# A four-layer attention kernel: maximum blocks of equal width, sums of two tiles in one run, three probability buffers, one buffer of rounded biases

## The reference

```python
x = x + attention_l(groupnorm(x))          # l = 0..3, 32 groups, no affine part

# attention_l, 12 heads of 16 channels, S = 2304 positions
q, k, v = split(x @ qkv_w + qkv_b)
attn = (q * scale) @ k.T + rel_h[..., :, None] + rel_w[..., None, :]   # rel_* = q . rel_pos tables
out = softmax(attn) @ v                    # per head
return concat_heads(out) @ proj_w + proj_b
```

## Time and profile before

| | us |
|---|---|
| median of 3 runs | 6808.28 (6807.99 to 6810.07) |
| profiled execution, span on the core | 6801.4 |
| PE busy | 6725.5 (99%) |
| DVE busy | 5454.7 (80%) |
| ACT busy | 4753.7 (70%) |
| POOL busy | 938.1 (14%) |
| mean granted PE clock | 0.996 of 2.4 GHz |

### The profile page before, as it was taken

How to read it: one execution, slowest core, us unless ns; L and a number is a source line. 1 busy time by engine, 2 the same in 40 slices (tenths; PEclk the granted TensorE clock), 3 DMA queues, 4 the chain that set the end, 5 groups by cost and what they waited for, 6 DMA issues and landing times.

```text
span 6801.4 us, 139326 instructions
## 1 busy us (share of the span) xinstructions
PE 6725.5 (99%) x53600; PEld 4245.8 (62%) x53600; DVE 5454.7 (80%) x9973; ACT 4753.7 (70%) x10225; POOL 938.1 (14%) x967
## 2 busy tenths in 40 slices
PE   7999999999999999999999999999999999999998
PEld 5666666666666666666665666666666666666664
DVE  7887888778887788877888778887888878888883
ACT  3776776767767777677776767767676676767775
POOL 2111010211112110121111210102101121101110
PEclk8999999999999999999999999999999999999999
DMA  6676676767677677667676766767677676777673
GB/s 164 148 156 152 137 160 138 163 151 142 152 144 168 144 143 156 149 158 149 142 155 149 158 143 143 161 145 166 140 144 157 147 165 138 143 152 156 144 154 88
DMA packets 306307, 1013.72 MB, mean 149 GB/s; under 512 B 107440, under 2 KB 196976, under 8 KB 215920
## 3 DMA queue, kind: packets, MB, share of 16 engines
q1 hardware_dynamic: 305648, 1004.81, 68.9%
HBM read 745.26 MB, written 255.69 MB: 147 GB/s over the span
## 4 chain that ended last, share of the span: by engine, by line
PE 96%; DMA 1%; DVE 1%; issue 0%; ACT 0%; SPq 0%; POOL 0%; DVEq 0%; ACTq 0%
PE work L805 30%; PE work L878 27%; PE work L796 27%; PE work L824 7%; PE work L843 3%; PE work L862 2%; PE work L851 1%; DMA moving<-rel_scratch 1%; DVE mpart L683 1%; PE work L830 0%; DVE xb L674 0%; ACT probs L561 0%; DMA back<-attention_scratch 0%; DVE hi L721 0%; PE work L835 0%
## 5 line engine op out<-in xcount | busy, mean ns | idle before, releaser
L683 DVE TENSOR_REDUCE mpart<-work 128x1 f32<-128x512 f32 (+1 forms) x8640 | 5088.7, 632 | 1079.7 <-PE work L805 1013.1
L561 ACT ACTIVATE probs<-work 128x512 f32<-128x512 f32 (+1 forms) x8640 | 4100.2, 564 | 866.6 <-PE work L796 852.1
L805 PE MATMUL work<-mkeys,hi 128*128 128x512 f32 (+1 forms) x8640 | 3404.1, 395 | 10.6 <-DVE mpart L683 8.8
L796 PE MATMUL work<-moving,keys 113*128 113x512 f32 (+1 forms) x8640 | 3299.9, 383 | 10.9 <-DMA moving<-rel_scratch 5.7
L805 PEld LDWEIGHTS work<-mkeys,hi 128*128 128x128 f32 x8640 | 1643.6, 190 | 622.4 <-DVE mpart L683 324.0
L878 PE MATMUL work<-probs,vall 128*17 128x288 f32 x27648 | 2013.1, 409 | 0.0
L796 PEld LDWEIGHTS work<-moving,keys 113*128 113x128 f32 x8640 | 1642.1, 190 | 362.3 <-ACT probs L561 39.2
L878 PEld LDWEIGHTS work<-probs,vall 128*17 128x17 f32 x27648 | 637.3, 96 | 846.8 <-ACT probs L561 358.3
L824 PEld LDWEIGHTS work<-image,tab 128*48 128x48 f32 x6912 | 401.6, 124 | 544.9 <-ACT probs L561 513.2
L490 POOL TENSOR_TENSOR full<-full,hi 128x384 f32<-128x384 f32 x576 | 583.5, 1016 | 938.7 <-DVE hi L721 937.6
L495 POOL TENSOR_TENSOR rden<-oraw,rden 128x576 f32<-128x576 f32 x96 | 137.1, 1428 | 3955.3 <-DMA rden<-inverse_scratch 3955.3
(11 more groups left out here) (42 smaller groups left out, 646.8 us busy)
## 6 DMA issues: line engine op xcount, KB each, us to landing
moving<-rel_scratch SPq DMA_DIRECT2D x1728, 144.0 KB
moving<-qk_scratch SPq DMA_DIRECT2D x288, 576.0 KB
rel_scratch<-hi SPq DMA_DIRECT2D x192, 432.0 KB, 5.7
rel_scratch<-full SPq DMA_DIRECT2D x192, 432.0 KB, 5.5
moving<-rel_scratch SPq DMA_DIRECT2D x288, 288.0 KB
image<-qk_scratch SPq DMA_DIRECT2D x384, 144.0 KB, 3.2
keys<-qk_scratch SPq DMA_DIRECT2D x192, 288.0 KB, 7.8
qk_scratch<-split_hi SPq DMA_DIRECT2D x144, 192.0 KB, 3.9
```

The source lines that it names most:

```text
L561: act.activation(probs[:, tile % RING, lo:up], bank[:, 0:up - lo], ACT.Exp).then_inc(act_read, 1)
L683: dve.tensor_reduce(mpart[:, u % 2, q, m:m + 1], bank[:, 0:MSPLIT[m][1] - MSPLIT[m][0]], AX.X, ALU.max)\
L796: pe.matmul(bank[:, 0:up - lo], tile_of(keys[0:K_ROWS, u % 2, :], c, third), moving[0:K_ROWS, slot_of(u, third)[0], lo:up], start=True, st ...
L805: pe.matmul(bank[:, 0:up - lo], hi[:, u % 2, q * P:(q + 1) * P], mkeys[:, u % 2, lo:up], start=True, stop=True).then_inc(for_dve, 1)
```

## The change

- `RING` goes from 2 to 3 and `hi` from two buffers to one, so the memory used stays the same.
- `MSPLIT` becomes five even blocks, 462 columns four times and 456 once, where it was 256 and then four times 512.
- `attend` runs at the end of even tiles only, for the two tiles before, in one run of 32 instructions.
- The rounding of biases moves from tiles 8 to 13 to tiles 8 to 12 and 14 (`HIGH_AT`), and waits for the store of the unit just before.
- SP stores `hi` in tile 15 (13 before) and `full` in tile 16 (14 before), there behind the loads of the next unit's last slot. The waits at line 540 and in `fullq_load` stay as they are.

```diff
-RING = 2
+RING = 3
-MSPLIT = SPLIT[-1:] + SPLIT[:-1]
+MAX_STEP = 2 * -(-N // (2 * MAXB))
+MSPLIT = [(MAX_STEP * i, min(MAX_STEP * (i + 1), N)) for i in range(MAXB)]
+HIGH_AT = (8, 9, 10, 11, 12, 14)
-        hi = sb("hi", [P, 2, N], F32R)
+        hi = sb("hi", [P, N], F32R)
...
-                    if t == 13 and u + 2 < UNITS:
+                    if t == 15 and u + 2 < UNITS:
                         sp.wait_ge(hi_ready, NB * (u + 3))
-                        rel_store(u + 2, hi[:, (u + 2) % 2, :].bitcast(F32), 0, rel_hi_stored)
+                        rel_store(u + 2, hi[:, :].bitcast(F32), 0, rel_hi_stored)
                     if t == 14 and 0 <= u + 1 < UNITS:
                         top_load(u + 1, 0)
-                    if t == 14 and u + 2 < UNITS:
-                        sp.wait_ge(lo_ready, NB * (u + 3))
-                        rel_store(u + 2, full[:, :], 1, rel_lo_stored)
...
                     if t == 16 and 0 <= u + 1 < UNITS:
                         slot_load(u + 1, 2)
                         top_load(u + 1, 2)
+                    if t == 16 and u + 2 < UNITS:
+                        sp.wait_ge(lo_ready, NB * (u + 3))
+                        rel_store(u + 2, full[:, :], 1, rel_lo_stored)
...
                 if r == 0:
                     dve.wait_ge(fullq_in, 32 * (u + 1))
-                    if u >= 2:
-                        dve.wait_ge(rel_hi_stored, 32 * (u - 1))
+                    if u >= 1:
+                        dve.wait_ge(rel_hi_stored, 32 * u)
...
-                        if 8 <= t < 14 and i == 2 and -2 <= u and u + 2 < UNITS:
-                            high(u + 2, t - 8)
+                        if i == 2 and t in HIGH_AT and -2 <= u and u + 2 < UNITS:
+                            high(u + 2, HIGH_AT.index(t))
...
-                        if i == SB and 0 < tile <= TILES * UNITS:
+                        if i == SB and tile % 2 == 0 and 0 < tile <= TILES * UNITS:
+                            attend(tile - 2)
                             attend(tile - 1)
```

More of the change, by code:

```diff
@@ L489, in low @@
                 pool.wait_ge(hi_ready, NB * u + r + 1)
-                pool.tensor_tensor(full[:, cols], full[:, cols], hi[:, u % 2, cols].bitcast(F32), ALU.subtract)\
+                pool.tensor_tensor(full[:, cols], full[:, cols], hi[:, cols].bitcast(F32), ALU.subtract)\
                     .then_inc(lo_ready, 1)
@@ L718, in high @@
                     dve.wait_ge(fullq_in, 32 * (u + 1))
-                    if u >= 2:
-                        dve.wait_ge(rel_hi_stored, 32 * (u - 1))
-                dve.tensor_copy(hi[:, u % 2, cols], full[:, cols]).then_inc(hi_ready, 1)
+                    if u >= 1:
+                        dve.wait_ge(rel_hi_stored, 32 * u)
+                dve.tensor_copy(hi[:, cols], full[:, cols]).then_inc(hi_ready, 1)
             def top(u):
@@ L804, in fill @@
                         pe.wait_ge(mkeys_in[u % 2], 32 * (u // 2 + 1))
-                    pe.matmul(bank[:, 0:up - lo], hi[:, u % 2, q * P:(q + 1) * P], mkeys[:, u % 2, lo:up],
+                    pe.matmul(bank[:, 0:up - lo], hi[:, q * P:(q + 1) * P], mkeys[:, u % 2, lo:up],
                               start=True, stop=True).then_inc(for_dve, 1)
```

## The result

| | before | after |
|---|---|---|
| median, us | 6808.55 | 7757.0 (7748.0 to 7773.0) |
| ratio to before, 95% interval | | 1.1398 (1.1384 to 1.1412) |
| span of the profiled execution, us | 6801.4 | 7750.8 |
| mean granted PE clock | 0.996 | 0.953 |

The account below looks back on a forecast made before the run. PE was taken to bound the kernel, with 96% of the span as its work, DVE next. 6808 + 50 (pairs) + 670 (store wait) + 232 (clock) = 7760 us, chance 0.56; range 7140 to 8030.

Parts of the forecast that it names:

- store: PE's lost time: ACT's first copy of a unit waits for the moved store; PE loses 7.2 us, 93 times: 670 us (310 to 790).
- clock: After PE's gap in the body, 5 us of work at clock 0.50, 93 times: 232 us (0 to 465).
- pairs, split, other moves: Sums of two tiles in one run let DVE hold PE up; even blocks cost nothing: +50 us in all.
- Issue and landing: Store of `full`: issued at T + 2.5, landed at T + 12.4; T is when tile 16's last score block is done.
- The low end: The second store takes the median 5.5 us from its issue, landing at T + 8.5; PE loses 3.3 us.
- The step from landing to block: In tile 0, from the stores' landing to PE's waiting score block: copy (0.49 us) and weight load, together 0.66 us.
- Rival B: Same store wait, cheaper: transfers overlap with the loads or the gap is too short for the clock; 7350 us, chance 0.31.
- nobody else waits for them: In a pair, only PE's score blocks and sums stand behind DVE's wait; a plain pair takes 0.28 us more.
- gain the 0.28 us: In the 43 units with projections DVE keeps up, so pairs get 0.28 us shorter; some 20 us off in all.
- The bound given for the term: For the pairs: -240 us if DVE never holds PE up, +240 if all are like the bare one.
- The even split: Maximum blocks: 2304 columns in five instructions as before, costing DVE what the old five cost; nothing by itself.
- C, D and E: No store wait: C, sums gain, 6570 us, 0.06; D, DVE holds PE, 6858, 0.04; E, both cancel, 6808, 0.03.

Follow-up runs that it names:

- the filled gap: The changed kernel with 24 unread maximum products added in tile 0, where PE waits: 7616.84 us, ratio 1.1182.
- the half exponential: The changed kernel with `full` stored in tile 14 again and ACT taking exponentials of only half of each score block: 6976.54 us, ratio 1.0255.
- half the reduction: The changed kernel with `full` stored in tile 14 again and DVE reducing only half of each maximum block: 6847.57 us, ratio 1.0053.

## Why the prediction was right, and where its terms were not

The forecast of 7760 us stands beside 7757. The mechanism of the store and the clock was right; that the sum fits to 3 us is luck: two errors of nearly the same size with opposite signs.

| term | forecast | measured | how |
|---|---|---|---|
| store: PE's lost time | 670 | 509 | third score block of tile 0 at T + 11.70 against T + 6.23, 93 times |
| clock | 232 | about 182 | the filled gap, 140 + 42 |
| store, not assigned | | 19 | 710 less the two |
| pairs, split, other moves | 50 | 239 | store back in tile 14 against before |

*Issue and landing.* Forecast T + 2.5 and T + 12.4; medians T + 3.9 and T + 11.2. The issue is later because the two loads that SP issues behind the stores of `hi` take 1.62 and 0.89 us to issue instead of 0.60 and 0.58. The landing is earlier because the term's rate was low (2.81 MB at 212 GB/s are 13.3 us, at the 218 to 237 of the stretches above 11.9 to 12.9) and because `hi` is issued 2.7 us before T, not 2.2. The low end, the median of 5.5 us behind the second store's own issue, was too short: that takes 6.8 us in after (medians; 6.5 in the kernel with the store alone moved, 5.8 with the store ahead of the loads). From the issue of the first of the two stores to the landing of the second it is 7.3, 7.0 and 7.3 us. That also shows what the runs leave open. The sum of the queued bytes, taken as in the prediction but at 228 GB/s, gives T + 10.9, T + 9.7 and T + 6.4 for the three; it is right within 0.3 us where loads stand ahead and 0.9 us short where they stand behind, so they may share the engines with the store. A delay of 7.2 us behind the first issue fits all three as well, within 0.2 us.

*What PE loses.* 7.2 forecast, 5.5 measured: the landing is 1.2 us earlier, and the score block that waits would have started at T + 6.2 in the mean, not T + 5.6: at T + 5.9 in most units and at T + 7.2 in 21, which carry a further projection in tile 17. The step from landing to block, 0.66 us, measured 0.61.

*The clock.* It fell, as forecast against the rival without it. 2.0 us a gap by the filled gap instead of 2.5: behind the 94 gaps it stayed at 0.50 for 4.5 us in the mean (3.3 in the place shown), not 5; half of 4.5, an estimate from the clock alone, is 2.2. The Trainium skill (TensorE: Matmul & The Clock Gate, "Why this matters for your kernels") warns of idle gaps in mid-kernel; the prediction had no row for one in the body; now there are some 95 in after, with the clock at 0.50 behind them, and the gaps of 2 us with the store ahead of the loads are shorter than those that the page warns of, where the measurement decides. Rival B's clause that "the gap is too short for the clock" fell by a wide margin, since the clock fell behind gaps of 2 us.

*The pairs: the step that failed.* In plain units 1.3 us forecast, 2.41 measured (mean of the 59 units). DVE's chain was priced right, as the half exponential shows, but the working left ACT out: "nobody else waits for them" was read on DVE's ring only. Of the 1.1 us missed, 0.52 are (1,2), where the two copies of the sums lost the sums of tile 1 as their cover, and 0.45 are (9,10), where the rounding behind POOL's work takes up to 1.6 us instead of 0.35. The sentence that projection units "gain the 0.28 us" had the wrong sign: 1.82 us are lost in each of the 21 with projections of queries and keys, by the reading above since ACT's copies of them sit in the ring of the scores, and 2.41 in each of the 28 with other projections (49 units in all; the prediction counts 43). In the seven units with the statistics of the groupnorm, which run on DVE, the loss is 6.28; with half the reduction these units gain 1.20 instead, so there it is DVE. 68 x 2.41 + 21 x 1.82 + 7 x 6.28 = 246, and the profiled executions differ by 246.7 (the medians by 239). The bound given for the term, +240, was reached.

*The even split* was costed at nothing, by DVE's equal sum, and cost about 25 us where each tile has its sums: its first block is 206 columns wider, so that DVE starts later in a tile. That this is the reason was not tried.

*The rivals.* C, D and E needed the store to land before T + 4.9; in after it never landed before T + 9.4. The kernel with the store in tile 14 is rival D without that condition: 7047, not 6858, again by the pairs.

## What to carry to other kernels

Before a store moves later, sum the bytes ahead of it on its queue and hold the landing against whoever may overwrite its source; when the slack is gone the wait costs twice, once as the gap and once as the low clock behind it. Before work is drawn together into a run, step through the run for every engine that empties PE's banks, the odd units included, and look for what the old order covered. A forecast that fits in the sum should be taken apart all the same: here the two terms of the store were 192 us too high together and that of the pairs 189 too low.

## What was not expected of the hardware

The low clock came behind gaps of 2 us: of the 64 gaps of 1.5 to 2.5 us in the kernel with the store at the front of tile 16, 57 were followed by work at 0.50. The gap took 143 us and the rest of the 263 is 120; half of the time at 0.50 behind the gaps, an estimate from the clock alone, is 106.

A rounding on DVE takes 0.35 us alone and 0.84 to 1.16 us in the two places shown, where POOL's subtraction runs; in both it ends 0.21 to 0.22 us after POOL's instruction does (817.72 against 817.51, 816.18 against 815.96). Of the 576 roundings with the store in tile 14, 450 start with POOL idle and take at most 0.36 us; 126 start while POOL runs some instruction, and end 0.22 us after it in the median. The Trainium skill (SBUF — State Buffer, "SBUF: two separate sides") says that the port pair that the two engines share is an exclusive lock: of an instruction of POOL and one of DVE in a two-port mode, whichever starts first has it for the whole instruction, and the other is blocked. The trace agrees; whether the rounding runs in such a mode no row tells.

The issue of tile 16's first load on SP grew from 0.60 to 1.62 us (medians 0.60 and 1.59) where 864 KB of stores had been issued just ahead. What SP waits for there no row tells.
